# A graph network sweep: who requests the line loads, the sync engine in its own order or ScalarE on its own queue

## What is computed

```python
xb = jnp.einsum('ei,bio->ebo', x[src], weight)          # 16 bases
msg = jnp.einsum('eb,ebo->eo', w_comp[etype], xb)       # 86 relations
x_hat = x[src] @ A1_w.T + A1_b
y_hat = x[dst] @ A2_w.T + A2_b + rel_emb[etype]
a = jnp.tanh(jax.nn.relu(jnp.sum(x_hat * y_hat, axis=-1) / scale))
nei = jax.ops.segment_sum(a[:, None] * msg, dst, num_segments=N)
```

## Time and profile before

| | |
|---|---|
| median of 3 runs | 1244.38 us (1241.84 to 1246.38) |
| the profiled execution | 1243.25 us, span from first to last instruction 1241.5 us |
| PE busy | 969.2 us (78%) |
| DVE busy | 997.3 us (80%) |
| ACT busy | 528.1 us (43%) |
| POOL busy | 633.9 us (51%) |
| transfers | 47.12 MB, 38 GB/s on average |

### The profile page before, as it was taken

How to read it: one execution, slowest core, us unless ns; L and a number is a source line. 1 busy time by engine, 2 the same in 40 slices (tenths; PEclk the granted TensorE clock), 3 DMA queues, 4 the chain that set the end, 5 groups by cost and what they waited for, 6 DMA issues and landing times.

```text
span 1241.5 us, 59214 instructions
## 1 busy us (share of the span) xinstructions
PE 969.2 (78%) x24732; PEld 901.6 (73%) x24732; DVE 997.3 (80%) x3020; ACT 528.1 (43%) x1339; POOL 633.9 (51%) x642
## 2 busy tenths in 40 slices
PE   2379898797886868787886868779436996899997
PEld 2368787786776767776775868668326996899996
DVE  8689999998889898898988989889435997555556
ACT  1145555554454544454544545445757970000000
POOL 5777777777777777777777777760000000000000
PEclk9578888887797888788787888878658997999999
DMA  4432222221222212221212222210000000000001
GB/s 110 73 71 46 53 49 48 51 47 47 49 47 51 47 47 49 47 51 47 50 46 50 47 50 47 50 46 30 4 15 2 4 4 3 4 4 4 4 4 17
DMA packets 56080, 47.12 MB, mean 38 GB/s; under 512 B 36901, under 2 KB 52011, under 8 KB 55809
## 3 DMA queue, kind: packets, MB, share of 16 engines
q1 hardware_dynamic: 35648, 32.93, 9.5%
q0 software_dynamic: 20160, 10.36, 6.2%
HBM read 40.94 MB, written 2.29 MB: 35 GB/s over the span
## 4 chain that ended last, share of the span: by engine, by line
PE 29%; DMA 22%; DVE 20%; SPq 14%; issue 13%; ACT 1%; DVEq 0%; POOLq 0%; ACTq 0%; POOL 0%
PE ps L821 13%; DMA arena<-line_table 11%; DMA agg_table<-arena 10%; PE ps L763 4%; SPq L520 4%; PE ps L729 4%; SPq L496 4%; SPq L521 2%; DVE arena L1257 2%; SPq L500 2%; DVE aggT L1298 2%; PE ps L698 2%; PE ps L710 2%; DVE arena L1286 2%; DVE arena L1452 2%
## 5 line engine op out<-in xcount | busy, mean ns | idle before, releaser
L588 POOL DMA_INDIRECT arena<-x_pad,arena x630 | 632.0, 1003 | 192.2 <-issue 188.9
L729 PE MATMUL ps<-arena 128*32 128x44 f32 (+3 forms) x7832 | 189.0, 221 | 147.3 <-DVE arena L1286 147.2
L729 PEld LDWEIGHTS ps<-arena 128*32 128x32 f32 x7832 | 139.1, 122 | 184.1 <-DVE arena L1286 154.5
L763 PE MATMUL ps<-aggT 128*128 128x128 bf16 x3192 | 239.5, 240 | 6.9 <-DVE aggT L1298 6.8
L821 PE MATMUL ps<-arena,adj_words 128*128 128x64 f16 (+1 forms) x6250 | 195.5, 193 | 36.9 <-DVEq L1402 33.7
L763 PEld LDWEIGHTS ps<-aggT 128*128 128x128 bf16 x3192 | 215.7, 110 | 8.2 <-DVE aggT L1298 8.2
L821 PEld LDWEIGHTS ps<-arena,adj_words 128*128 128x128 fp8e4 x6250 | 193.4, 98 | 38.9 <-DVEq L1402 34.4
L1286 DVE TENSOR_TENSOR arena<-ps,arena 128x768 f32<-128x768 f32 x196 | 187.9, 959 | 6.7
L1257 DVE TENSOR_SCALAR arena<-pair_no,arena 128x275 bf16<-128x275 f16 (+2 forms) x784 | 177.1, 294 | 0.0
L998 ACT ACTIVATE adj_words<-arena 128x500 uint8 x196 | 126.3, 644 | 82.2 <-issue 80.2
L710 PE MATMUL ps<-arena 128*128 128x175 bf16 (+3 forms) x1567 | 143.4, 239 | 4.7 <-DVE arena L1257 4.5
(11 more groups left out here) (212 smaller groups left out, 1143.7 us busy)
## 6 DMA issues: line engine op xcount, KB each, us to landing
arena<-line_table SPq DMA_DIRECT2D x28, 602.0 KB
arena<-x_pad,arena POOLq DMA_INDIRECT x630
arena<-pick_table SPq DMA_DIRECT2D x38, 128.0 KB
arena<-line_table SPq DMA_DIRECT2D x28, 140.0 KB
arena<-dst_parts SPq DMA_DIRECT2D x196, 5.7 KB
agg_table<-arena SPq DMA_DIRECT2D x196, 2.5 KB
dst_parts<-aggT SPq DMA_DIRECT2D x1, 735.0 KB, 14.6
x<-x_pad SPq DMA_DIRECT2D x1, 400.0 KB
```

The source lines that it names most:

```text
L588: pool.indirect_dma_start(to, None, table, bass.IndirectOffsetOnAxis(ap=index, axis=0)).then_inc(done, 16)
L729: return nc.tensor.matmul(to.rearrange("p (d m) -> p d m", m=MIX_COLS)[:, :, 0:m1 - m0], rows_of_slot, factors[:, :, m0:m1], start=False, ...
L763: mm = nc.tensor.matmul(ps[:, at:at + PICK_WIDE * FEAT], pick_hot[:, j, k * P:(k + 1) * P], x_parts[:, t, j * PICK_WIDE:(j + 1) * PICK_WID ...
```

## The change

The two transfers of a chunk's lines are issued by ScalarE on its own queue. `load_lines` takes the engine as an argument. SP still requests chunk 0 before the sweep. ScalarE requests chunk 1 as the sweep begins, and chunk c + 1 at group 7c, right behind the group's tanh, after waiting that 7c groups are fetched. SP's loop keeps the codes, the side loads and the stores in their order.

```diff
+        def load_lines(eng, c):
+            of = slice(c * LINE * WINDOW, (c + 1) * LINE * WINDOW)
+            eng.dma_start(lines[0:RELS, c % 2, :], line_table[0:1, of].to_broadcast([RELS, LINE * WINDOW]))\
+               .then_inc(line_in[c % 2], 16)
+            eng.dma_start(lines[RELS:SIDE, c % 2, :], line_table[1:2, of].to_broadcast([PAGE, LINE * WINDOW]))\
+               .then_inc(line_in[c % 2], 16)
+
@@ sync
-            def load_lines(c):
...
-            load_lines(0)
+            load_lines(sp, 0)
@@ sync, run_sweep
                 for g in range(GROUPS):
-                    if g % LINE == 0:
-                        c = g // LINE
-                        if c >= 2:
-                            sp.wait_ge(fetched, (c - 1) * LINE)
-                        if c >= 1:
-                            load_lines(c)
@@ scalar, run_sweep
                 act.wait_ge(sweep_cleared, 1)
+                act.wait_ge(lines_stored, 16)
+                load_lines(act, 1)
@@ scalar, run_sweep
                     a.activation(weight_e[:, g % 2, :], score[:, g % 2, :], ACT.Tanh, scale=1.0 / sqrt(FEAT))\
                      .then_inc(weight_ready, 1)
+                    if g % LINE == 0 and g >= LINE and g // LINE + 1 < LINES:
+                        act.wait_ge(fetched, g)
+                        load_lines(act, g // LINE + 1)
                     copy_counts(g)
```

## The result

| | before | after |
|---|---|---|
| median | 1243.75 us (4 runs, 1241.84 to 1246.38) | 1194.66 us (4 runs, 1193.75 to 1199.62) |
| ratio | | 0.9612, 95% interval 0.958 to 0.9644 |
| the profiled execution | 1243.25 us, span 1241.5 | 1199.62 us, span 1197.8 |

The change takes 49.1 us off; 55.6 were forecast (1188). The profiled execution of the changed kernel is the longest of its four, 5 us over their median.

What follows compares the result with a forecast made beforehand. VectorE's pace bounds the sweep, but SP, stalled by stores, sets it after 252 us. From 1243.25 us, -42.8 (sweep, limited by gathers) and -12.8 (its end) give 1187.7, stated as 1188; 8-in-10 range 1174 to 1228.

Steps and rivals of the forecast that it cites:

- SP is held by a store behind the line load: Sweep: once per chunk SP stalls some 10 us for a small store queued behind the line load, setting the pace.
- Not because it is long: Line load in the sweep: it is late because SP comes late to it, not because of its length.
- The request comes early enough: ScalarE's line request: load there after 17.2 to 19.9 us, against 19.5 to 22.3 us from tanh to `make_lines`.
- lengthen by 2.0 to 2.8 us: Line load on ScalarE's queue: sharing DMA engines with other traffic was taken to add this to its landing time.
- The stores pass the load on another queue: SP's small stores no longer wait for the line load; SP then needs 18.8 us per chunk against VectorE's 27.6.
- rival A: SP's small transfers still wait for the line load, saving only 16 us: 1227 us; chance 12%.
- waits for stores under 30 us: Sign of a right forecast: SP's waits for its stores fall from 246 us to under 30.
- ScalarE pays 0.6 us per chunk, covered: ScalarE's two requests per chunk cost 0.6 us, covered by its 0.69 us idle before the tanh.
- GpSimd's gathers take over at group 145: Late sweep: VectorE eats the gathers' lead by group 145, so the sweep shortens by 42.8 us, not 55.
- one turn of 137.8 us: VectorE's undisturbed time for 35 groups, from one window, taken as its pace throughout the sweep.
- A delay at the start is covered by the gathers' slack: Sweep start: any small delay from chunk 1's load beside chunk 0's is covered by 12 us of slack.
- The end of the sweep gives 12.8: After the sweep: VectorE's wait for the sums shrinks, gaining 12.8 us, the limit set by ScalarE's wait for VectorE.

Runs made afterwards that it cites:

- e4: Kernel before, lines uncut on SP; each store goes to its own rows and waits for the fourth store before it: 1185.6 us.
- e3: Kernel before, SP still requesting all line loads, with the 86-row request cut into 80 and 6 rows: 1184.3 us.
- e10: Kernel before with SP's 86-row line request cut into 85 and 1 rows: 1182.8 us in one run.
- e8: Changed kernel with ScalarE's line request made two groups later (g % 7 == 2): 1272.4 us.
- e6: Changed kernel with four more 4-byte requests on ScalarE behind each of its line loads from chunk 2 on: 1219.9 us.
- e1: Changed kernel, but chunk 1 is requested by SP at its group 7 as before; ScalarE requests chunks 2 to 27: 1186.4 us.
- e2: Changed kernel with ScalarE's 86-row line request cut into 80 and 6 rows: 1186.0 us.
- e7: Kernel before with only chunk 1 requested by ScalarE as the sweep begins; chunks 2 to 27 stay with SP: 1256.6 us.

## Why the prediction was right or wrong

- *SP is held by a store behind the line load.* Right, and shown from two sides: the store's wait loosened (e4), the load shortened (e3, e10), each without the change and each with a gain of 57 to 61 us. The prediction's "Not because it is long" doesn't stand beside it: that the load is long is what holds the store, and it left the cause of the length unasked. One reading on the way was off: of the 67 GB/s over the 16 us of the load, the load is 742 KB / 16 us = 46 and not 51, so 21 and not 16 are left for the gathers; the conclusion from it stays.
- *The request comes early enough.* Right. No line wait after chunk 0, with 19.7 us at the least against a load of 16.6 at the most; e8 shows what the same queue is worth when it is late. The load does not lengthen by 2.0 to 2.8 us beside SP's traffic as assumed, but by under 1.
- *The stores pass the load on another queue.* Right in kind, half in size. They do pass (rival A is out), at 5.7 us a store instead of 2.7. The sign that was named, waits for stores under 30 us, is missed with 163.3. SP was taken to need 18.8 us for a chunk; with its waits for stores it needs 18.8 + 163.3 / 26 = 25 of the 28, and the 88.6 us of waiting for VectorE, 3.4 per chunk, are the rest. By the Trainium skill's page "DMA: Bandwidth & Descriptors", section "Queues, rings and completion order", each engine takes turns between queues; the 5.7 us agree with turns, the 11.8 on one queue with standing behind. The sentence in its section "Issuing engines are not separate DMA queues" that requests on several engines save issue time alone doesn't hold here: the time saved is SP's wait for the store.
- *ScalarE pays 0.6 us per chunk, covered.* The size was right (0.59). The slack over it is about half a microsecond (e6).
- *GpSimd's gathers take over at group 145.* Wrong. The changed kernel never waits for one. Where the start isn't late, VectorE waits for one at groups 184 and 185 in e1 (2.8 us) and between 190 and 195 in e3 (2.5 us), and the profiles of e2, e4 and e10 show no such wait. The step that failed is the pace of VectorE: one turn of 137.8 us was taken for all, and the four later ones average 140.0. That leaves 9 us of the 55 that VectorE was to gain, and with it the lead that the gathers were to lose. The two errors cancel: the last scores were forecast at 838.6, and where nothing else disturbs they are at 835.8 to 838.0 (e1 to e4). That this number came out is luck, and so is a part of the small distance between 1188 and 1194.7.
- *A delay at the start is covered by the gathers' slack.* Wrong, and the largest term missing: 12.4 us in the trace, 8.2 between the medians of the changed kernel and e1. The prediction called the delay small and looked only at chunk 0's load beside it; what stood in the way, by the landings in four kernels, was the 735 KB store of `dst_parts`, a step that it named nowhere. And since most of the slack wasn't there, little hid it: of the 12.7 us between the first scores of the changed kernel and of e1, 9.7 are left at the last scores.
- *The end of the sweep gives 12.8.* Mostly right: 9.3. SP still issues its 24 last stores without a pause from 822.96 to 862.5, since it is not as far ahead as assumed. Where SP is free (e4) VectorE waits only 7.9 us for the sums, and the limit by ScalarE's degrees is reached (VectorE waits 2.6 us for it).

The sum: 1188 forecast, 1194.7 measured, and 1186.4 without the late start.

## What to carry to other kernels

Before moving a request to another queue, ask why it is long and what waits behind it: here the cause was a row count of 86, and taking it to 80 + 6 or 85 + 1 on the old queue gave 10 us more than the move, 8 of them because the move also made one load start too early. When a long transfer is made to start earlier, look at every transfer in flight at its new time, on every queue. And a pace read from one undisturbed window is one sample: several windows, or their spread, belong in the sum.

## What the runs showed of the hardware

A load of 602 KB in rows of 7168 bytes kept 2 packets under way with 86 rows on its request, 5 with 85, 16 with 80 and 1 with 43 + 43. From its request to VectorE's work on it passed 14.6 to 16.5 us with 86 rows; the last row packet ended after 7.6 to 9.3 us with 85 + 1 and 4.7 to 6.2 with 80 + 6, and after 26 to 28 with 43 + 43, where VectorE waited 13.5 us per chunk. A store of 2.5 KB issued behind the long load on its queue let its successor go after 11.8 us, on the other queue beside it after 5.7. A request can also stand at its own issue: SP's codes took 9.75 us to issue while a 735 KB store of short rows stood ahead of it on its queue and a long load ran on ScalarE's (8.22 in e7, 0.49 in e1); why it stands is not shown. The small load behind that store reached TensorE's fetch 0.5 to 0.8 us after the store's landing, in four kernels. A request of 4 bytes costs ScalarE 0.35 us (1.41 for four), one of 602 KB 0.47.
